# Cross attention with a mixture of experts on one Trainium2 core: middle rows fetched during the expert stage, a result buffer for each batch, last stage unrolled

## The reference

```python
mid = x + attention(layernorm(x), ctx)        # two cross attentions, mixed by sigmoid(alpha), Wout, bout
h = layernorm(mid)
probs = softmax(h @ gate_w.T)                 # 16 experts
w, idx = top_k(probs, 4); w = w / sum(w)
y_e = (silu(h @ w1[e]) * (h @ w3[e])) @ w2[e] # expert e, inner width 128
out = mid + sum over the 4 chosen e of w_e * y_e
```

## Time and profile before

| | |
|---|---|
| median of 3 runs | 2157.95 us (2154.18 to 2159.37) |
| the profiled execution, its own time | 2155.32 us |
| its span in the profile | 2153.5 us |
| busy in the span: PE, DVE, ACT, POOL | 1907.1, 1417.3, 1261.0, 1211.3 us |
| moved by DMA | 210.54 MB |

### The profile page before, as it was taken

One profiled execution on the slowest core, in us unless ns is written; L12 is line 12 of the kernel. 1 busy time (PEld: TensorE's weight loads), 2 busy tenths in 40 slices (PEclk: granted clock), 3 DMA queues, 4 the chain that ended last, 5 costly groups with the idle time before them and its releaser, 6 DMA issues.

```text
span 2153.5 us, 53309 instructions
## 1 busy us (share of the span) xinstructions
PE 1907.1 (89%) x15778; PEld 1642.3 (76%) x15779; DVE 1417.3 (66%) x3205; ACT 1261.0 (59%) x3605; POOL 1211.3 (56%) x1683
## 2 busy tenths in 40 slices
PE   5999999999999999999999999999369999999100
PEld 4788888888888878888888888878269999999100
DVE  4567666667666666766666766666536666666577
ACT  4766666676666666666666666667136556555100
POOL 2466666566666566666566666556426666666200
PEclk9999999999999999999999999999679999999655
DMA  5610111101111110111101111110766666666798
GB/s 149 153 36 35 42 49 47 34 34 34 39 49 49 34 34 34 39 45 48 39 34 34 38 45 49 39 34 26 189 158 184 180 182 179 184 184 179 276 371 317
DMA packets 158596, 210.54 MB, mean 98 GB/s; under 512 B 24273, under 2 KB 131425, under 8 KB 158562
## 3 DMA queue, kind: packets, MB, share of 16 engines
q1 hardware_dynamic: 119394, 127.75, 20.7%
q0 software_dynamic: 26112, 71.86, 9.2%
q10 hardware_dynamic: 13056, 10.50, 1.7%
HBM read 113.02 MB, written 97.03 MB: 98 GB/s over the span
## 4 chain that ended last, share of the span: by engine, by line
PE 82%; DMA 7%; issue 3%; DVE 3%; SPq 3%; POOL 2%; ACT 1%; DVEq 0%; POOLq 0%; ACTq 0%
PE p_s L1047 12%; PE p_av L1145 12%; PE p_pt L1129 12%; PE p_s L1111 10%; PE p_gu L1300 9%; PE p_x L1180 5%; PE p_y L1318 4%; PE p_s L1057 4%; DMA z<-mid_rows 3%; PE p_xt L1289 3%; DMA out_dram<-z 2%; PE p_x L1047 2%; PE p_pt L1047 2%; PE p_av L1057 2%; PE p_pt L1057 2%
## 5 line engine op out<-in xcount | busy, mean ns | idle before, releaser
L512 POOL TENSOR_TENSOR probs<-probs,inv 128x256 f32<-128x256 f32 x1024 | 596.0, 614 | 434.0 <-DVE inv L844 433.3
L603 ACT ACTIVATE probs<-p_s,nmx 128x256 f32<-128x256 f32 x1024 | 475.3, 488 | 67.5 <-DVE nmx L837 62.7
L837 DVE TENSOR_REDUCE nmx<-p_s 128x4 f32<-128x1024 f32 x256 | 313.1, 1223 | 140.3 <-PE p_s L1111 136.7
L544 POOL DMA_INDIRECT y_rows<-y_out,xg x288 | 276.3, 959 | 177.8 <-issue 107.9
L504 POOL DMA_INDIRECT x_rows<-routed,slot_i x256 | 252.5, 986 | 170.0 <-DVE target L829 95.8
L1129 PEld LDWEIGHTS p_pt<-ident,probs 128*128 128x128 f32 x2048 | 222.2, 141 | 87.5 <-issue 62.4
L1129 PE MATMUL p_pt<-ident,probs 128*128 128x128 f32 x2048 | 280.0, 280 | 7.5 <-issue 4.9
L1145 PE MATMUL p_av<-probsT,val 128*64 128x256 f32 x2048 | 280.0, 394 | 6.5 <-DVE probsT L741 5.8
L741 DVE COPY probsT<-p_pt 128x512 f32<-128x512 f32 x256 | 176.1, 688 | 109.8 <-PE p_pt L1129 107.1
L1047 PE MATMUL p_s<-rowsT_hi,wp_hi 128*128 128x256 f32 x768 | 231.6, 302 | 8.3 <-DVE wp_lo L857 8.3
L591 ACT COPY probsT<-p_pt 128x512 f32<-128x512 f32 x256 | 152.5, 596 | 137.4 <-PE p_pt L1129 117.3
(11 more groups left out here) (183 smaller groups left out, 4712.5 us busy)
## 6 DMA issues: line engine op xcount, KB each, us to landing
xg<-x_rows SPq DMA_DIRECT2D x144, 257.0 KB
y_in<-y_rows SPq DMA_DIRECT2D x32, 1024.0 KB, 6.7
rows<-in_ctx_dram SPq DMA_DIRECT2D x32, 256.0 KB, 2.7
x_in<-in_x_dram SPq DMA_DIRECT2D x32, 256.0 KB, 2.7
mid_rows<-x_mid SPq DMA_DIRECT2D x32, 256.0 KB, 2.2
z<-mid_rows SPq DMA_DIRECT2D x32, 256.0 KB, 7.4
out_dram<-z ACTq DMA_DIRECT2D x32, 256.0 KB, 5.7
y_rows<-y_out,xg POOLq DMA_INDIRECT x288
```

The source lines that it names most:

```text
L512: pool.tensor_tensor(pr[:, h, t, :], pr[:, h, t, :], rc[:, g:g + 1].to_broadcast([P, S]), ALU.mult).then_inc(normed_p, 1)
L544: pool.indirect_dma_start(y_rows, bass.IndirectOffsetOnAxis(ap=xg[r][:, i, D:D + 1].bitcast(I32), axis=0), y_out[r % 4][:, i, :], None).th ...
L603: act.activation(probs[u % 2][:, h, t, :], p_s[:, 2 * (u % 2) + h, t * S:(t + 1) * S], ACT.Exp, bias=nmx[u % 2][:, g:g + 1], accum_out=sum ...
L837: dve.tensor_reduce(nmx[i][:, :], p_s[:, 2 * i:2 * i + 2, :].rearrange("p h (t k) -> p (h t) k", t=ST), AX.X, ALU.max, negate=True).then_i ...
```

## The change

1. `late_slot` is given a narrower life, and 24 tiles `z_ahead` (2 KB a partition each, 48 KB in all) take its place in SBUF. During the expert stage, right behind the loads of groups 8 to 31, SP loads the middle rows of batches 0 to 23 into them, on the same queue. SP first waits for `mid_stored` and `late_lo`; the loads count on one semaphore, `z_back`.
2. In the last stage each batch has a tile `z` of its own: 24 of them `z_ahead`, 8 more beside. `y_in` keeps four buffers, placed above the held rows. Batches 24 to 31 still load their `z` there, behind their `y_in`.
3. SP issues the load of `y_in` for batch b when DVE is done with batch b-4 (`z_step`), and no longer when that batch's store has landed. ACT waits for all stores once, at the end.
4. The last stage is written out batch by batch on SP, DVE and ACT, without hardware loops, and so are the loads of groups 8 to 31 on SP. The attention stage and the expert stage's other engines are as before.

```diff
+    Z_AHEAD = 24
...
+            with ExitStack() as loading:
+                late_slots = [sb(f"late_slot{i}", [P, PIECE], stack=loading)[:, :] for i in range(E // 2 + E // 4)]
+
+            z_ahead = [sb(f"z_ahead{i}", [P, ST, D], stack=later) for i in range(Z_AHEAD)]
...
+            sb("z_held", [P, Z_AHEAD * ST * D], stack=last)
             y_in = [sb(f"y_in{i}", [P, ST, TOP_K, D], stack=last) for i in range(4)]
-            z = [sb(f"z{i}", [P, ST, D], stack=last) for i in range(4)]
+            z = z_ahead + [sb(f"z{b}", [P, ST, D], stack=last) for b in range(Z_AHEAD, B)]
...
-            with sp.Fori(1, GROUPS // LOADS) as q:
+            def next_group(q, r):
+                wait_alone(sp, xg_t, LOADS * (q - 1) + r + 1)
+                sp.wait_ge(y_sent[r % 4], 32 * (2 * q + r // 4 - 1))
+                load_group(LOADS * q + r, r)
+            def load_z(b, landed):
+                sp.dma_start(z[b][:, :, :], mid_dram[b]).then_inc(landed, 16)
+            sp.wait_ge(mid_stored, 16 * B)
+            sp.wait_ge(late_lo, LATE)
+            for q in range(1, Z_AHEAD // LOADS + 1):
                 for r in range(LOADS):
-                    wait_alone(sp, xg_t, LOADS * (q - 1) + r + 1)
-                    sp.wait_ge(y_sent[r % 4], 32 * (2 * q + r // 4 - 1))
-                    load_group(LOADS * q + r, r)
+                    next_group(q, r)
+                    load_z(LOADS * (q - 1) + r, z_back)
+            with sp.Fori(Z_AHEAD // LOADS + 1, GROUPS // LOADS) as q:
+                for r in range(LOADS):
+                    next_group(q, r)
...
-            if B > 4:
-                with sp.Fori(1, B // 4) as q:
-                    for r in range(4):
-                        sp.wait_ge(out_stored[r], 16 * q)
-                        sp.dma_start(y_in[r][:, :, :, :], y_dram[4 * q + r]).then_inc(y_back[r], 16)
-                        sp.dma_start(z[r][:, :, :], mid_dram[4 * q + r]).then_inc(y_back[r], 16)
+            for b in range(B):
+                if b >= 4:
+                    sp.wait_ge(z_step, ST * TOP_K * (b - 3))
+                sp.dma_start(y_in[b % 4][:, :, :, :], y_dram[b]).then_inc(y_back[b % 4], 16)
+                if b >= Z_AHEAD:
+                    load_z(b, y_back[b % 4])
...
+            for b in range(B):
+                act.wait_ge(z_step, ST * TOP_K * (b + 1))
+                act.dma_start(out_dram[b], z[b][:, :, :]).then_inc(out_stored, 16)
+            act.wait_ge(out_stored, 16 * B)
...
+            for b in range(B):
+                dve.wait_ge(y_back[b % 4], 16 * (b // 4 + 1 + max(0, (b - Z_AHEAD) // 4 + 1)))
+                if b == 0:
+                    dve.wait_ge(z_back, 16 * Z_AHEAD)
                 for k in range(TOP_K):
                     for t in range(ST):
                         if k:
                             dve.wait_ge(z_step, ST * TOP_K * b + ST * k + t - 1)
-                        dve.scalar_tensor_tensor(z[r][:, t, :], y_in[r][:, t, k, :],
-                                                 share[:, bass.ds(ST * b + t, 1), k], z[r][:, t, :],
+                        dve.scalar_tensor_tensor(z[b][:, t, :], y_in[b % 4][:, t, k, :],
+                                                 share[:, ST * b + t, k:k + 1], z[b][:, t, :],
                                                  ALU.mult, ALU.add).then_inc(z_step, 1)
```

More of the change, by code:

```diff
@@ L161, in xattn_moe_kernel @@
         with ExitStack() as later:
-            late_slots = [sb(f"late_slot{i}", [P, PIECE], stack=later)[:, :] for i in range(E // 2 + E // 4)]
+            with ExitStack() as loading:
+                late_slots = [sb(f"late_slot{i}", [P, PIECE], stack=loading)[:, :] for i in range(E // 2 + E // 4)]
+            z_ahead = [sb(f"z_ahead{i}", [P, ST, D], stack=later) for i in range(Z_AHEAD)]
             wgu_lo = sb("wgu_lo", [P, E, KT, 2, I], F32R, later)
@@ L220, in xattn_moe_kernel @@
         y_back = [sem(f"y_back{i}") for i in range(4)]
-        out_stored = [sem(f"out_stored{i}") for i in range(4)]
+        z_back = sem("z_back")
+        out_stored = sem("out_stored")
         consts_set, al_set, early_hi, early_lo, middle_hi, late_lo, gate_t, gate_hi, gate_lo = new(
@@ L448, in _ @@
                 load_group(r, r)
-            with sp.Fori(1, GROUPS // LOADS) as q:
-                for r in range(LOADS):
-                    wait_alone(sp, xg_t, LOADS * (q - 1) + r + 1)
-                    sp.wait_ge(y_sent[r % 4], 32 * (2 * q + r // 4 - 1))
-                    load_group(LOADS * q + r, r)
+            def next_group(q, r):
[7 more added lines that the diff above has]
+            for q in range(1, Z_AHEAD // LOADS + 1):
+                for r in range(LOADS):
+                    next_group(q, r)
[3 more added lines that the diff above has]
+                    next_group(q, r)
             for i in range(4):
                 sp.wait_ge(y_sent[i], 32 * (GROUPS // 4))
-            sp.wait_ge(mid_stored, 16 * B)
-            for r in range(4):
-                sp.dma_start(y_in[r][:, :, :, :], y_dram[r]).then_inc(y_back[r], 16)
-                sp.dma_start(z[r][:, :, :], mid_dram[r]).then_inc(y_back[r], 16)
-            if B > 4:
-                with sp.Fori(1, B // 4) as q:
-                    for r in range(4):
-                        sp.wait_ge(out_stored[r], 16 * q)
-                        sp.dma_start(y_in[r][:, :, :, :], y_dram[4 * q + r]).then_inc(y_back[r], 16)
-                        sp.dma_start(z[r][:, :, :], mid_dram[4 * q + r]).then_inc(y_back[r], 16)
+            for b in range(B):
[4 more added lines that the diff above has]
+                    load_z(b, y_back[b % 4])
         @block.gpsimd
@@ L1000, in _ @@
             stage_b(dve, group, before=1, after=2)
-            def total(b, r, loads):
-                dve.wait_ge(y_back[r], loads)
+            for b in range(B):
+                dve.wait_ge(y_back[b % 4], 16 * (b // 4 + 1 + max(0, (b - Z_AHEAD) // 4 + 1)))
+                if b == 0:
+                    dve.wait_ge(z_back, 16 * Z_AHEAD)
                 for k in range(TOP_K):
```

## The result

The changed kernel takes 2125.82 us (median of 4 runs, 2123.23 to 2128.78), the kernel before 2158.23 us in the same comparison (2154.18 to 2159.37). The ratio is 0.9850 by the medians; by the comparison of the runs it is 0.9852, with a 95% interval of 0.9836 to 0.9868. That is 32 us faster, where 19 were forecast, and outside the range given (2130 to 2149). The profiled execution has a span of 2127.0 us against 2153.5, 26.5 us less; its own time, 2128.78 us, is the highest of the four. The traces can therefore account for 26.5 us and not for all 32.

A forecast was written before the change was run, and what follows sets the result against it. It took PE to bound most of the kernel and the DMA engines the last stage. Terms -17.8 - 2 + 1 = -18.8 us took 2157.95 to 2139.2, rounded to 2139, range 2130 to 2149.

The forecast's parts named there:

- The bound: Last stage: DMA engines taken as the bound at share 1.02 and 366 GB/s, with DVE not the bound.
- The `y_in` load no longer waits for a store: Last stage: dropping the store from a buffer's cycle gains small gaps and part of the drain, 2 us, bounds 0 and 4.
- The 24 `z` loads: Last stage: 24 loads leaving it save 17.8 us at 0.74 us each, bounds 17.2 and 26.5.
- The estimate of 15.8 us: Last stage: worth of the 24 z loads by the skill's fixed 3 cycles a packet; the trace's price was preferred.
- DVE stays below both, so it stays hidden: Last stage: DVE's 3.26 us a batch stay under the DMAs' 3.58 and 4.3 us, so DVE costs nothing.
- the forecast's own signs of being wrong: PE waits on `xg` of several us, gaps in DVE's row with data landed, or a last stage on DVE's 3.26 us.
- DVE becomes the bound, the DMAs gain more: Rival, last stage: without the store in the cycle it falls to DVE's floor, 112.7 us, whole time 2126, chance 0.08.
- The expert stage, 1 us: Expert stage: the added z loads make an odd group's rows late, costing 1 us, bounds 0 and 9.
- Neither slower rival: Expert stage, late groups: moderate, 9 us, 2147, chance 0.10; as in the saturated end, 32 us, 2170, chance 0.03.
- the late fetch of straight code: Rival, last stage: written-out code fetched late through full DMA engines, costing 0 to 5 us, some 2143, chance 0.06.
- The median: Whole kernel: 18.8 us taken off the median of 2157.95 gives 2139.2; the profiled execution stands 2.6 us below the median.
- The signs named ahead: Last stage about 126 us near 366 GB/s, batches every 3.6 then 4.3 us, DVE's load waits about 30 us.

The follow-up runs named there:

- e1: Changed kernel with no middle rows fetched ahead, all 32 z loads back in the last stage, still no store wait: 2470.58 us, ratio 0.9961 to the kernel before.
- e9: Kernel before with 8 buffers for y_in and z in place of 4 in the last stage, store wait kept: 2454.15 us, ratio 0.9959.
- e2: Changed kernel with the wait on stores put back before y_in loads, middle rows still fetched ahead: 2478.42 us, ratio 1.0002 to the kernel before.
- e10: Changed kernel with y_in of batch b issued only when DVE is done with batch b-2: 2484.15 us, ratio 1.0062 to the kernel before.
- e4: Kernel before with its last stage written out without hardware loops, buffers, waits and loads unchanged: 2473.57 us, ratio 0.9995.
- e11: Changed kernel with its 24 z loads spread over the expert stage and the other 8 issued early in the last stage: 2430.88 us, ratio 0.9852.
- e12: Changed kernel with a z load behind every group load 8 to 143, not the first 24, 136 in all: 2444.59 us, ratio 0.9852.

## Why the prediction was wrong

- **The bound.** The forecast read a share of 1.02 as "DMA is the bound there, DVE is not", and of SP's 93.2 us of waiting for stores it said "that alone would prove nothing: the engines are full while it waits". This is the step that failed. The share counts the time that packets take, not what the engines could carry: 1.02 went with 366 GB/s before, and 1.05 with 407 in `e1` and `e9`, which move the same bytes.
- **The term that failed: "The `y_in` load no longer waits for a store", bounds 0 and 4 us, 2 taken.** Alone it is worth 145.1 - 132.4 = 12.7 us (`e1`), and on top of the loads fetched ahead 137.2 - 115.4 = 21.8 us (`e2` against the change). In the forecast's own order the sum should have read -17.0 - 12.7 + 3.2 = -26.5 us, the difference of the spans, where it read -17.8 - 2 + 1 = -18.8.
- **What stood there to be read.** The chain of waits of the kernel before shows one buffer's round in plain rows:

```profile
2034.82 0.37 SPq L468
2035.38 6.98 DMA z<-mid_rows
...
2045.94 5.79 DMA out_dram<-z
2051.89 0.37 SPq L468
2052.45 7.05 DMA z<-mid_rows
...
2063.08 5.71 DMA out_dram<-z
2068.95 0.37 SPq L468
```

  Load, DVE, store, next load: 17.07 us from 2034.82 to 2051.89, 17.06 to the next (the four rounds after it take 16.6 to 18.4). Four buffers share a round, so a batch takes 17.07 / 4 = 4.27 us and 32 of them 137 us. That is no second piece of evidence beside the 50.3 MB at 366 GB/s: 1.573 MB in 4.27 us is that rate. The round alone does not say which of the two is the cause either, since it closes in `e1` as well, at 407 GB/s. It should have made the length of the round a theory of equal rank; `e9` and `e10` show that it was the cause. One view of before does point that way, the rate in 40 slices of the stretch, here 2010 to 2130 us before and then 2350 to 2450 us of `e1`:

```profile
GB/s 369 405 404 394 338 297 380 387 405 419 344 301 416 323 341 416 331 358 409 407 389 390 324 405 345 351 417 337 302 417 324 341 417 374 357 364 207 371 420 355
...
GB/s 417 404 405 407 406 408 410 398 409 413 404 410 407 395 419 408 396 420 400 404 411 406 406 415 401 406 408 403 408 410 398 420 396 403 414 411 399 415 405 403
```

  Before, the rate swings between 207 and 420 GB/s, so the engines did carry 400 and more in many slices. In `e1` it stays between 395 and 420. The other traces divide the same way: `e4`, `e2` and `e10`, where the round was the limit, fall to 188 GB/s and less in single slices; `e9`, `e11` and the change's first 24 batches stay above 370.
- **The 24 `z` loads, 17.8 us.** Right in size where the DMA engines are the bound: `e1` to the change is 132.4 - 115.4 = 17.0 us. Under the old round they bring only 7.9 us (`e2`). The two parts do not add up: 12.7 and 7.9 alone, 29.7 together, since either is held back by the other's limit. The sum in the forecast added them as if they were independent. The estimate of 15.8 us that was worked out from the Trainium skill (DMA: Bandwidth & Descriptors, "Why small descriptors are slow") is 1.2 us below the 17.0, the stores' price 0.8 above it.
- **DVE.** Its 3.26 us a batch were right; back to back it is 3.17. "DVE stays below both, so it stays hidden" was not: it works for 76.09 us without a gap, and the 1.311 MB of a batch at 412 GB/s take 3.18 us, the same within 0.01. A last stage on DVE's pace was among the forecast's own signs of being wrong, and for batches 0 to 23 it came.
- **The rival "DVE becomes the bound, the DMAs gain more", 2126, chance 0.08.** Its mechanism is the one that the runs bear out: the store in the buffer's cycle kept the mean at 366, and without it the stage comes down to DVE's pace for 24 batches, with the DMA engines' limit right beside it (`e11`). Its number is in part luck. It gave the stage 112.7 us, measured are 115.4, and it had no delay of the stage's start, measured are 3.2 us; these 5.9 us are made up by the 5.9 us by which the medians differ more than the traces do. That "there was always work in the queues", which I held against it, is what a share of 1.02 cannot show.
- **The expert stage, 1 us.** The changed kernel's last stage starts 3.2 us later. A group's load takes 3.6 us to land in the median of the whole stage and 4.1 in the stretch with the `z` loads, where I had reckoned with 2.2 to 2.7, and the DMA share in 1597 to 1664 us is 0.86, forecast 0.9. In that stretch PE issued 538 matmuls where it had issued 565, about one group less. SP's load of group 8 went out 0.7 us sooner than before and that of group 31 1.9 us later, so most of the delay arose there. That rows came late is not seen: of PE's waits in the stretch, 0.2 us are put down to `xg`, once. On the other chips `e12` found no such cost; what remains open is whether the `z` loads did it at a period of 2.8 us, or whether one execution of each kernel is too little to tell. Neither slower rival came about, nor the late fetch of straight code: DVE's first 192 instructions of the stage run without a gap.
- **The median.** The spans differ by 26.5 us, the medians by 32.4. The rest is where the two profiled executions lie among the others: the one before is 2.9 us below its median, the one after 3.0 above. In which stage the other executions were shorter or longer no trace shows.
- **The signs named ahead.** Forecast were a last stage of about 126 us near 366 GB/s, batches every 3.6 us and then 4.3, and 30 us of DVE's waits for loads. Measured are 115.4 us, 412 and 396 GB/s, 3.17 and then 3.92 us, and 19.1 us (13.6 + 5.5).

No version tried is clearly faster than the change. `e11_spread_and_mixed` has the lowest median of its series, 5.4 us below the change, with overlapping runs and the same last stage.

## What to carry to other kernels

Before a DMA share near 1 is taken as the bound, follow one buffer once round in the chain of waits. If load, work, store and next load close a round whose length over the number of buffers is the observed period, the depth may be the bound and the bandwidth in the row its result. The round cannot decide this by itself: in `e1` it closes too, with a longer load in it. Two things did decide it here. The rate in short slices swung where the round was the limit and was even where it was not, and doubling the buffers (`e9`), which moves no byte more, raised GB/s at nearly the same share. And two edits that each lift one of two limits on the same stage are costed by the limit that is left after both, not by adding what each would bring alone.

## What the runs showed of the hardware

The 16 DMA engines' share did not tell 366 from 407 GB/s. The DMA queues over a stretch of each show where the time went, first the kernel before as read for the forecast (120 us: 85.3% for 37.13 MB is 2.76 us a MB on SP's queue, 2.87 on ACT's), then `e1_own_z_no_ahead` in 2350 to 2450 us, with the same mix of loads and stores:

```profile
q1 hardware_dynamic: 14076, 33.97, 85.7%
q10 hardware_dynamic: 6955, 6.70, 19.1%
```

Here SP's queue takes 85.7 / 33.97 = 2.52 us a MB and ACT's 19.1 / 6.70 = 2.85. The stores' packets cost the same, the loads' packets were 9% dearer when fewer loads were queued. It is not the chip: the unrolled kernel before (`e4`) has 2.72 us a MB on SP's queue on the chip of `e1`. Why a load's packet takes longer in a shallow queue was not settled here. At two loads deep (`e10`) the share fell as well, to 0.82 at 290 GB/s; with the wait for stores and fewer bytes (`e2`) to 0.92 at 334.
